# Attention units of the first phase: the product with the values moved next to the scores on TensorE, its copy and normalisation moved into the same unit

## What is computed

```python
# layer 0: queries are the normalised rows, keys and values are the context
qh, kh, vh = _split_heads(q), _split_heads(encoder_k), _split_heads(encoder_v)   # 16 heads of width 8
scores = jnp.einsum('bhqd,bhkd->bhqk', qh, kh) + encoder_attention_mask
weights = jax.nn.softmax(scores, axis=-1)
ctx = jnp.einsum('bhqk,bhkd->bhqd', weights, vh)
return jax.nn.relu(ctx @ wo_w.T + wo_b)
# layer 1: q, k, v are projected, scores scaled, clipped to +-100 and masked
scores = jnp.where(mask == 0, -jnp.inf, jnp.clip(scores, -100.0, 100.0))
out = jnp.einsum('bhqk,bhkd->bhqd', jax.nn.softmax(scores, axis=-1), v)
```

## Time and profile before

| | before |
|---|---|
| median of 3 runs | 2442.34 us (2441.18 to 2447.15) |
| the profiled execution's own time | 2443.1 us |
| its span, first to last instruction | 2441.3 us |
| PE, DVE, ACT busy over the whole span | 1941.3, 1508.2, 1294.3 us |
| first phase: first to last start of a scores matmul | 41.9 to 968.7 us |
| mean granted TensorE clock over the span | 0.882 of full speed |

### The profile page before, as it was taken

One profiled execution on the slowest core, in us unless ns is written; L12 is line 12 of the kernel. 1 busy time (PEld: TensorE's weight loads), 2 busy tenths in 40 slices (PEclk: granted clock), 3 DMA queues, 4 the chain that ended last, 5 costly groups with the idle time before them and its releaser, 6 DMA issues.

```text
span 2441.3 us, 49251 instructions
## 1 busy us (share of the span) xinstructions
PE 1941.3 (80%) x17184; PEld 1549.6 (63%) x17184; DVE 1508.2 (62%) x3920; ACT 1294.3 (53%) x4431; POOL 628.8 (26%) x626
## 2 busy tenths in 40 slices
PE   3887977878689878447788889898998887878864
PEld 2666866667577656135666667776776766666664
DVE  5886865757567788555566665655656554555442
ACT  2755554545455656435576756565665654544421
POOL 0002021311411220013233343242342423232331
PEclk9877999879899987557799999898998999999987
DMA  7002444343344200310000011122221222222253
GB/s 212 28 16 89 121 123 128 101 125 106 112 139 120 67 22 6 113 41 17 26 6 13 6 56 50 50 66 77 66 66 49 74 76 79 74 83 78 76 153 107
DMA packets 125124, 184.17 MB, mean 75 GB/s; under 512 B 10320, under 2 KB 82064, under 8 KB 124624
## 3 DMA queue, kind: packets, MB, share of 16 engines
q1 hardware_dynamic: 116688, 164.23, 22.8%
q0 software_dynamic: 8192, 16.79, 2.4%
HBM read 145.52 MB, written 35.45 MB: 74 GB/s over the span
## 4 chain that ended last, share of the span: by engine, by line
PE 34%; DVE 9%; ACT 6%; issue 6%; POOL 1%; DMA 1%; SPq 0%; DVEq 0%; ACTq 0%; POOLq 0%
PE ps L1610 6%; PE ps L1859 4%; ACT pb L1999 4%; PE ps L1838 3%; PE ps L1845 3%; PE ps L1648 3%; PE ps L1632 2%; DVE nm L2351 2%; PE ps L1639 2%; PE ps L1621 2%; PE ps L1817 2%; PE ps L1666 1%; DVE hT L2142 1%; ACT pt L2007 1%; DVE hT L2137 1%
## 5 line engine op out<-in xcount | busy, mean ns | idle before, releaser
L1999 ACT ACTIVATE pb<-ps,nm 128x128 f32<-128x128 f32 x1024 | 363.3, 377 | 264.1 <-DVE nm L2351 263.9
L2040 POOL TENSOR_TENSOR pb<-pb,rcs 128x512 f32<-128x512 f32 x256 | 266.7, 1042 | 803.8 <-DVE rcs L2340 802.3
L964 ACT ACTIVATE pb<-pb,nm 128x128 f32<-128x128 f32 x1024 | 313.0, 391 | 92.6 <-DVE nm L1187 90.3
L2351 DVE TENSOR_REDUCE nm<-ps 128x8 f32<-128x1024 f32 x128 | 156.1, 1219 | 138.3 <-PE ps L1845 71.5
L2360 DVE COPY pt<-ps 128x512 f32<-128x512 f32 x128 | 88.3, 690 | 223.0 <-PE ps L1859 223.0
L1999 ACT ACTIVATION_READ_ACCUMULATOR pb<-ps,nm 128x1 f32 x1024 | 222.0, 217 | 0.0
L1859 PE MATMUL ps<-w,pb 128*128 128x128 f32 x1024 | 173.9, 297 | 49.8 <-ACT pt L2007 42.7
L1610 PE MATMUL ps<-hT,big 128*128 128x128 f32 x960 | 151.8, 308 | 54.7 <-DVE hT L2142 44.1
L851 PE MATMUL ps<-w,pb 128*128 128x128 f32 x1024 | 168.9, 309 | 28.7 <-ACT pb L964 18.6
L1610 PEld LDWEIGHTS ps<-hT,big 128*128 128x128 f32 x960 | 135.4, 216 | 80.1 <-DVE hT L2142 58.4
L1859 PEld LDWEIGHTS ps<-w,pb 128*128 128x128 f32 x1024 | 128.2, 153 | 80.8 <-issue 68.0
(11 more groups left out here) (365 smaller groups left out, 4387.8 us busy)
## 6 DMA issues: line engine op xcount, KB each, us to landing
big<-in_we SPq DMA_DIRECT2D x92, 514.0 KB
big<-in_we SPq DMA_DIRECT2D x120, 384.0 KB
big<-sorted_in SPq DMA_DIRECT2D x8, 960.0 KB, 6.5
sorted_out<-big SPq DMA_DIRECT2D x28, 256.0 KB
sorted_in<-big SPq DMA_DIRECT2D x4, 1472.0 KB, 12.1
sorted_out<-h_all SPq DMA_DIRECT2D x16, 256.0 KB
hidden<-h_all SPq DMA_DIRECT2D x7, 512.0 KB, 2.9
h_all<-hidden SPq DMA_DIRECT2D x7, 512.0 KB, 3.9
```

What stands on the lines that cost most here:

```text
L964: m = a.activation(pb[:, n % 2, k * S:(k + 1) * S], pb[:, n % 2, k * S:(k + 1) * S], ACT.Exp, bias=nm[:, n % 2, k:k + 1])
L1999: m = a.activation(pb[:, n % 2, e * S:(e + 1) * S], ps[:, score_bank(n) + half, k * S:(k + 1) * S], ACT.Exp, bias=nm[:, n % 2, e:e + 1], a ...
L2040: g_.tensor_tensor(p4, p4, r4.unsqueeze(2).to_broadcast([P, 4, S]), ALU.mult).then_inc(n2["p_normed"], 1)
L2351: v.tensor_reduce(nm[:, n % 2, :], ps[:, bank:bank + 2, :].rearrange("p a (j k) -> p (a j) k", k=S), AX, ALU.max, negate=True).then_inc(n2 ...
```

## The change

On PE the product(n-2) and the turn of ou(n-3) move from behind `work(1)` to directly behind scores(n), ahead of `work(0)`. The transposes(n-1) are emitted in halves with `work(1)` between them. On ACT the copy to `ou` takes unit n-2 instead of n-3 and moves behind the copy of the first half of pt(n-1). On DVE the normalisation takes unit n-3 instead of n-4 and moves from ahead of mask and maximum(n) to behind them. Which semaphores are waited for stays as it was, apart from the unit numbers. No instruction is added or removed.

```diff
@@ TensorE, turn n (scores(n) stand above, unchanged)
-                    work(0, n)
-                    if 0 <= n - 1 < NUN:
-                        p = n - 1
-                        for k in range(BLK):
-                            if k % 4 == 0:
-                                pe.wait_ge(s["exps"], 2 * p + 1 + k // 4)
-                                if p:
-                                    pe.wait_ge(s["p_lo" if k else "p_hi"], p)
-                            m = pe.transpose(ps[:, 2 + k // 4, (k % 4) * S:(k % 4 + 1) * S],
-                                             pb[:, p % 2, k * S:(k + 1) * S], ident)
-                            if k % 4 == 3:
-                                m.then_inc(s["transposed"], 1)
-                    work(1, n)
                     if 0 <= n - 2 < NUN:
...
                         m.then_inc(s["o_turned"], 1)
-                    work(2, n)
+                    work(0, n)
+                    for half in range(2):
+                        if 0 <= n - 1 < NUN:
+                            p = n - 1
+                            pe.wait_ge(s["exps"], 2 * p + 1 + half)
+                            if p:
+                                pe.wait_ge(s["p_lo" if half else "p_hi"], p)
+                            for k in range(4 * half, 4 * half + 4):
+                                m = pe.transpose(ps[:, 2 + half, (k % 4) * S:(k % 4 + 1) * S], pb[:, p % 2, k * S:(k + 1) * S],
+                                                 ident)
+                            m.then_inc(s["transposed"], 1)
+                        work(1 + half, n)
@@ ScalarE
-                    if 0 <= n - 3 < NUN:
-                        p = n - 3
-                        a.wait_ge(s["pv"], p + 1)
-                        if p:
-                            a.wait_ge(s["normed"], p)
-                        a.activation(ou[:, :], ps[:, 4, 0:2 * S], ACT.Copy).then_inc(s["o_read"], 1)
                     if 0 <= n - 1 < NUN:
...
                         a.activation(pt[:, p % 2, 0:4 * S], ps[:, 2, :], ACT.Copy).then_inc(s["p_hi"], 1)
+                    if 0 <= n - 2 < NUN:
+                        p = n - 2
+                        a.wait_ge(s["pv"], p + 1)
+                        if p:
+                            a.wait_ge(s["normed"], p)
+                        a.activation(ou[:, :], ps[:, 4, 0:2 * S], ACT.Copy).then_inc(s["o_read"], 1)
@@ VectorE
-                    if 0 <= n - 4 < NUN:
-                        p = n - 4
...
-                            .then_inc(s["normed"], 1)
                     if n < NUN:
...
                         v.tensor_reduce(nm[:, n % 2, :], buf, AX, ALU.max, negate=True).then_inc(s["maxed"], 1)
+                    if 0 <= n - 3 < NUN:
+                        p = n - 3
...
+                            .then_inc(s["normed"], 1)
```

More of the change, by code:

```diff
@@ L1187, in _ @@
                         v.tensor_reduce(nm[:, n % 2, :], buf, AX, ALU.max, negate=True).then_inc(s["maxed"], 1)
+                    if 0 <= n - 3 < NUN:
+                        p = n - 3
+                        j, u = divmod(p, NU)
+                        b, c = divmod(u, 2)
+                        turned = ps[:, 4, 2 * P:4 * P].rearrange("p (k d) -> p k d", d=32)
+                        v.wait_ge(s["o_turned"], p + 1)
+                        v.reciprocal(rc[:, :], turned[:, :, DH]).then_inc(s["o_recip"], 1)
+                        v.wait_ge(s["o_recip"], p + 1)
+                        if u == 0 and j >= 2:
+                            v.wait_ge(s["oT_psum"], j - 1)
+                        v.tensor_tensor(os_[j % 2][:, b, c * 64:(c + 1) * 64].rearrange("p (k d) -> p k d", d=DH),
+                                        turned[:, :, 0:DH], rc[:, :].unsqueeze(2).to_broadcast([P, BLK, DH]), ALU.mult)\
+                            .then_inc(s["normed"], 1)
                     work(1, n)
```

## The result

The changed kernel is slower: 2487.03 us, median of 5 runs (2481.73 to 2501.77), against 2442.34 us. The ratio is 1.0191 with a 95% interval of 1.0166 to 1.0216, some 45 us. A time 18 us shorter had been forecast. The profiled execution is the slowest of the five, 2501.77 us, so its figures are 15 us above the median.

What follows compares the result with a forecast made beforehand. PE was busiest, 80% of the span, with DVE close to the bound outside the tiles. 0 - 16 - 7 + 4 + 1 = -18 us from 2443.1 gave 2425, 2424 us for the median; range 2412 to 2434, 8 in 10 2400 to 2450.

Steps and rivals of the forecast that it cites:

- step 5: In 84 units exponentials, waiting for the maximum, come 0.94 us later; DVE's copy of pt's second half isn't covered; +1 us.
- step 2: PE's 30.4 us wait for the copy to ou goes; a little over half comes back, -16 us.
- Step 1: Loop of a unit without other work: product and turn leave, normalisation and copy to ou enter; 0.
- Step 3: Product and turn cover PE's place-0 DMA waits, -3 us, and waits for ACT's evacuation, -4 us.
- Step 4: Place-0 hidden items on PE come 0.92 us later, making DVE's mask 0.46 us late in 8 cases; +4 us.
- the slower rival: Late exponentials hold DVE's copy of pt's second half outside the tiles; 12 to 30 us, 2455 us, worst 2465; chance 0.18.
- The clock's rival: Fewer PE gaps raise the granted clock, 16 us besides the 18; 2400 to 2408 us; chance 0.10.
- The signs: Wrong if DVE's copy L1192 newly waits over 15 us, scores wait about 30 us for the mask, or tile time stays.

Runs made afterwards that it cites:

- second pair: The kernel before and the changed kernel, both unchanged, traced again on another chip; 2449.33 us for the kernel before, ratio 1.0136 for the changed one.
- second trace: The changed kernel, unchanged, traced again on another chip; 1.0136 of the kernel before.
- mended variants: Variants of the changed kernel with ACT's work(1) ahead of its copy to ou; 1.0049 with split transposes, 0.9958 with whole ones.
- g4_work0_first: From c_work_first_unsplit, PE's work(0) moved ahead of product and turn; 1.0067 of the kernel before.
- a4_work_first: The changed kernel with ACT's work(1) moved ahead of its copy to ou; 1.0049 of the kernel before.
- c_work_first_unsplit: The changed kernel with ACT's work(1) ahead of its copy to ou and PE's transposes whole, work(1) behind them; 0.9958, repeated 0.9960, of the kernel before.
- a3_unsplit: The changed kernel with the transposes whole again and PE's work(1) behind both halves; 1.0186 of the kernel before.

## Why the prediction was wrong

Two steps failed: step 5, which left out what stands on ACT between the copy to ou and the exponentials, and step 2, whose gain was taken up by another wait at the same place.

- **The bound.** Right that both loops, PE's and DVE's, are close and that the tile stretch is where PE has most to do. There the changed kernel waits more, 29 us, and works at a lower clock, 25 us.
- **Step 1, the bare unit, 0.** Nearly right: after the tiles 1 us came back, and ahead of them 6.7 us were lost, 6.2 in the second pair, which no step had. Some 2 us of them are gone by the fifth unit, whose mask starts at 62.05 us instead of 60.02.
- **Step 2, -16 us from the vanished wait for ou. This step failed by its size.** The wait did vanish. But 31.1 us of waiting for DVE's second copy stand at the same matmuls (48.7 in the second trace, 29.6 to 33.7 in the mended variants). The gain measured at the product is about nothing instead of 16 us. The prediction named this wait as something "at most" to be seen and gave it no price. The copy stands on DVE behind maximum and normalisation, and PE, coming straight from the scores, is early for it.
- **Step 3, cover, -7.** Its direction is shown by g4_work0_first: with `work(0)` ahead instead, 1.1 points are lost, though through DVE's wait for the turn, which the step did not have. The DMA waits did fall, from 15.1 to 8.3 us (6.7 to 3.6 in the second pair). The other half did not come: PE's wait for ACT's evacuation of tiles rose from 4.6 to 7.3 us.
- **Step 4, place-0 tiles, +4.** Not visible: DVE's wait for the tiles' matmuls fell, from 95.8 to 85.8 us.
- **Step 5, late exponentials, +1. This is the step with the hole.** It followed the 0.94 us between maximum and exponentials only to the exponentials. But ACT's `work(1)` stands between the copy to ou and the exponentials, and was shifted by the whole way from normalisation ahead of the mask to normalisation behind the maximum: from 0.94 to 3.22 us after the mask's start, in the turn shown. In the diff `work(1)` is an unchanged line, and in the ACT rows of a unit without other work it doesn't appear. a4_work_first gives 0.9 to 1.4 points for exactly this, 21 to 34 us, and c_work_first_unsplit against a3_unsplit 2.3 points. For the exponentials themselves the step was right: ACT's wait for the maximum fell from 90.3 to 6.2 us, and PE did not wait longer for them. The split is in no term of the sum; only the slower rival names items between the halves, at 1 us each. It is worth 0.5 points by itself and 0.9 in the mended kernel.
- **The rivals.** The slower one had the right sign and partly the right place: DVE's wait at its copy did appear, 95.7 us with remote ones against 12.4 us. But a3_unsplit took most of it away without any gain. Its price, 12 to 30 us, was weighed on units without other work, and 54 us were lost where there is other work. The clock's rival went the other way: 0.91 to 0.85 in the tile stretch, and 0.81 and 0.68 to 0.80 and 0.65 in the two stretches of the earlier trace rows ahead of it.
- **The signs.** That L1192 waits over 15 us for transposes was named as a sign of being wrong, and it does, 81.3 us. PE's wait for the mask ahead of the scores rose too, from 1.9 to 18.6 us, short of the 30 named.

With both found losses out the kernel is 0.4% (8 to 10 us) faster than the one before, about half of the 18 forecast, and part of that may be ACT's new order and not the change.

## What to carry to other kernels

When an operation is moved behind a later one of its engine, list everything that stands behind its consumer on the consumer's queue, also lines that the diff shows as unchanged, and take the row from the stage with the most other work, not from the barest one. A wait that goes may only have covered the next: ask which semaphore of the same instruction is satisfied last once the first is early. And work for others (evacuations of a single buffer) goes ahead of an operation that waits for a long chain, not behind it: on one chip, with the split undone in both, that one moved line made the difference between 1.9% slower and 0.4% faster.

## What the runs showed that I had not expected

The kernel before took 2344 to 2449 us, depending on the chip: medians of 2442.34, 2347.03, 2448.98, 2437.74 and 2344.28 us in five sets, while repeated runs within a set mostly stayed within 1%. The second and the fifth set are the same chip. The ratios of c_work_first_unsplit, 0.9958 and 0.9960, agree across that gap.

The traces say where the gap lies. In all ten traces from the slower chips DVE and ACT wait, for 113 to 159 us together in the first phase, on something that the profile can only call remote; in the seven from the fastest chip there is no such wait. In the longest of them PE passes single matmuls 0.7 us apart, with idle time that the profile puts down to issue (kernel before, up to 500.5 us, and in six more of the ten at some place between 474 and 521 us):

```profile
499.79 0.37 PE L869 MATMUL ps<-pt,h_all 128*9 128x128 f32 x1 [0.33 <-issue]
500.50 1.22 DVE L572 TENSOR_TENSOR pb<-ps,mask1i 128x1024 f32<-128x1024 f32 x1 [17.81 <-remote]
```

What PE lacks there is not shown. Both kernels have these stretches, so waits that stem from them are not to be charged to the change: the 9.5 us for L903 are one, ACT having stood 20.35 us on such a wait just before.

And an order on three engines is not a sum. The split costs 0.45% in the old order and 0.9% in the mended one, and in the changed kernel nothing that a comparison across chips can show. Moving PE's product costs 8.5% without the copy's and normalisation's move, where with them, and ACT's place-1 work ahead, the whole is 0.4% faster.
